# One core, a GNN and linear-attention layer with experts: V·K products and feature folds written as pairs of 64 columns or 64 rows of the TensorE array, the folds in two PSUM banks of their own

## What is computed

```python
q = split_heads(x @ Wq.T + bq)
k = split_heads(x @ Wk.T + bk)
v = split_heads(x @ Wv.T + bv)
q_prime = _feature_map(q, P)          # relu(einsum('bhsd,hmd->bhsm', t, P)) / sqrt(64)
k_prime = _feature_map(k, P)
kv = jnp.einsum('bhsm,bhsd->bhmd', k_prime, v)
attn = jnp.einsum('bhsm,bhmd->bhsd', q_prime, kv)
```

## Time and profile before

| What | us |
|---|---|
| median of 3 runs | 1213.19 (1212.43 to 1213.55) |
| the profiled execution | 1213.78 |
| its span, first to last instruction | 1211.8 |
| TensorE busy (matmuls) | 1133.4, 94% of the span |
| TensorE weight loads | 979.1, 81% |
| VectorE, ScalarE, GpSimd busy | 384.5, 250.0, 293.6 |
| folds (L1491), busy time | 34.5, 256 records |
| kv (L1574), busy time | 22.1, 160 records |

### The profile page before, as it was taken

How to read it: one execution, slowest core, us unless ns; L and a number is a source line. 1 busy time by engine, 2 the same in 40 slices (tenths; PEclk the granted TensorE clock), 3 DMA queues, 4 the chain that set the end, 5 groups by cost and what they waited for, 6 DMA issues and landing times.

```text
span 1211.8 us, 15068 instructions
## 1 busy us (share of the span) xinstructions
PE 1133.4 (94%) x5547; PEld 979.1 (81%) x5547; DVE 384.5 (32%) x1007; ACT 250.0 (21%) x388; POOL 293.6 (24%) x236
## 2 busy tenths in 40 slices
PE   3999999999999989999889986888799999999998
PEld 3886888878899988888668875667599999998887
DVE  5865255655531011322202112333532112111111
ACT  4431111112233343211101111322312211112000
POOL 5001201122132254300134423233303332216000
PEclk9999999999999999999989998999899999999999
DMA  5222001212243565512387766665103212114321
GB/s 190 96 69 96 12 18 54 68 57 70 64 129 108 196 241 197 168 41 98 89 263 221 221 178 187 196 181 165 53 2 113 70 56 64 57 56 166 121 96 70
DMA packets 143364, 139.28 MB, mean 115 GB/s; under 512 B 6507, under 2 KB 120507, under 8 KB 142012
## 3 DMA queue, kind: packets, MB, share of 16 engines
q1 hardware_dynamic: 141996, 135.51, 35.7%
q10 hardware_dynamic: 1296, 2.79, 0.6%
HBM read 102.32 MB, written 35.96 MB: 114 GB/s over the span
## 4 chain that ended last, share of the span: by engine, by line
PE 84%; DMA 6%; DVE 4%; ACT 3%; issue 2%; SPq 2%; DVEq 0%; ACTq 0%
PE ps L1481 9%; PE ps L1483 9%; PE ps L1482 9%; PE ps L1745 6%; PE ps L1747 6%; PE ps L1746 6%; DMA qs0L<-qT_d 3%; PE ps L1791 3%; PE ps L1792 3%; PE ps L1793 3%; PE ps L1661 3%; PE ps L1687 3%; PE ps L1682 3%; PE ps L1663 3%; PE ps L1662 3%; PE ps L1491 2%
## 5 line engine op out<-in xcount | busy, mean ns | idle before, releaser
L1481 PE MATMUL ps<-w_hi,xnH 128*128 128x512 f32 x480 | 192.2, 400 | 0.0
L1483 PE MATMUL ps<-w_hi,xnL 128*128 128x512 f32 x480 | 188.4, 392 | 0.0
L1482 PE MATMUL ps<-w_lo,xnH 128*128 128x512 f32 x480 | 188.2, 392 | 0.0
L1483 PEld LDWEIGHTS ps<-w_hi,xnL 128*128 128x128 f32 x480 | 90.7, 189 | 19.4
L1481 PEld LDWEIGHTS ps<-w_hi,xnH 128*128 128x128 f32 x480 | 91.2, 190 | 17.9
L1482 PEld LDWEIGHTS ps<-w_lo,xnH 128*128 128x128 f32 x480 | 91.2, 190 | 17.8
L751 POOL TENSOR_TENSOR cL<-cR,cH 128x1280 fp32r<-128x1280 f32 x20 | 58.7, 2937 | 145.5 <-ACT cH L967 132.8
L701 POOL TENSOR_TENSOR acc<-acc,cw 128x320 f32<-128x320 f32 x40 | 35.4, 884 | 172.9 <-ACT cw L873 172.1
L1604 PE MATMUL ps<-xnH,w_hi 128*128 128x416 f32 (+1 forms) x192 | 70.2, 366 | 3.4 <-DVE mL L1264 3.3
L1745 PE MATMUL ps<-x2H,guH 128*128 128x416 f32 (+1 forms) x192 | 69.4, 362 | 0.4 <-ACT wT L1046 0.4
L1747 PE MATMUL ps<-x2H,guL 128*128 128x416 f32 (+1 forms) x192 | 69.0, 359 | 0.0
(11 more groups left out here) (310 smaller groups left out, 2083.4 us busy)
## 6 DMA issues: line engine op xcount, KB each, us to landing
cR<-c_d SPq DMA_DIRECT2D x20, 640.0 KB, 4.4
foldin<-in SPq DMA_DIRECT2D x32, 256.0 KB, 2.7
guR<-in SPq DMA_DIRECT2D x16, 512.0 KB, 5.2
c_d<-cw SPq DMA_DIRECT2D x40, 160.0 KB
w_raw<-in SPq DMA_DIRECT2D x12, 512.0 KB, 6.7
xb<-in SPq DMA_DIRECT2D x10, 512.0 KB, 5.0
qs0H<-qT_d SPq DMA_DIRECT2D x10, 512.0 KB, 6.2
qs0L<-qT_d SPq DMA_DIRECT2D x10, 512.0 KB, 7.4
```

The source lines that it names most:

```text
L1481: pe.matmul(target, xnH[:, kc, cols], wH[w][:, kc, :], start=(kc == 0), stop=False)
L1482: pe.matmul(target, xnH[:, kc, cols], wL[w][:, kc, :], start=False, stop=False)
L1483: mm = pe.matmul(target, xnL[:, kc, cols], wH[w][:, kc, :], start=False, stop=(kc == KC - 1))
```

## The change

`fold` and `kv` issue eight f32 matmuls in place of four, each for one head. In `fold` a matmul has the 64 rows of its head as contraction (`tile_position` (0, 0) or (64, 0)), still 128 columns of weights, and 64 moving columns. In `kv` it has all 128 rows, but 64 columns of weights, which go to the left or the right half of the array (`tile_position` (0, 0) or (0, 64)), and 64 moving columns. The two row halves of a fold write into two different banks, which belong to the folds alone: 6 and 7 for f = 0, 0 and 1 after that. The folds leave the rotation of three banks and get semaphores of their own; a fold waits until VectorE has drained the fold before it. kv writes 64 partitions by 64 columns of bank 5 per head, and `kv_out` copies the same elements from there. The index transposes of the edge ranges move from banks 6 and 7 to 5.

```diff
@@ _job_ids
             names.append(("v", hf, t))
-            if 1 <= t <= KC:
-                names.append(("fold", hf, t - 1))
...
-        names.append(("fold", 3, j) if j < KC else ("m", (j - KC) // 2, (j - KC) % 2))
+        if j >= KC:
+            names.append(("m", (j - KC) // 2, (j - KC) % 2))
...
+        def fold_banks(f):
+
+            first = 0 if f else 6
+            return ps[:, first * BANK:(first + 2) * BANK].rearrange("q (k b) -> q k b", k=2)[:, :, 0:4 * HD]\
+                .rearrange("q k (g m) -> q k g m", g=4)
+
+        def fold_panel(w, kc):
+            return w[:, kc, :].rearrange("q (g k m) -> q k g m", g=4, k=2)
...
             def fold_high(f, kc):
-                name = ("fold", f, kc)
-                act.wait_ge(*made(name))
-                act.activation(wH[(1, 1, 0, 1)[f]][:, kc, :], job_bank(name), ACT.Copy).then_inc(fold_hi, 1)
+                act.wait_ge(fold_mm, fold_index(f, kc) + 1)
+                act.activation(fold_panel(wH[(1, 1, 0, 1)[f]], kc), fold_banks(f), ACT.Copy).then_inc(fold_hi, 1)
...
             def fold(f, kc):
-                name, n = ("fold", f, kc), fold_index(f, kc)
-                free_bank(name)
+                n, banks = fold_index(f, kc), fold_banks(f)
+                if n:
+                    pe.wait_ge(fold_lo, n)
+                else:
+                    pe.wait_ge(bias_ev, 1)
                 pe.wait_ge(in_fold[n % 2], 16 * (n // 2 + 1))
                 for g in range(4):
-                    mm = pe.matmul(job_bank(name)[:, g * P:(g + 1) * P], foldin[:, n % 2, g, :],
-                                   pbd_s[:, f % 2 * 4 + g, :], start=True, stop=True)
-                mm.then_inc(mm_done, 1)
+                    for k in range(2):
+                        own = slice(k * HD, (k + 1) * HD)
+                        mm = pe.matmul(banks[:, k, g, :], foldin[own, n % 2, g, :], pbd_s[own, f % 2 * 4 + g, own],
+                                       start=True, stop=True, tile_position=(k * HD, 0))
+                mm.then_inc(fold_mm, 1)
...
                 for g in range(4):
-                    mm = pe.matmul(bank(5)[:, g * P:(g + 1) * P], vst[:, t, g * P:(g + 1) * P],
-                                   ktmp[:, t % 2, g * P:(g + 1) * P], start=(t == 0 and g == 0),
-                                   stop=(t == NT - 1 and g == 3))
+                    for k in range(2):
+                        head = slice(g * P + k * HD, g * P + (k + 1) * HD)
+                        mm = pe.matmul(bank(5)[k * HD:(k + 1) * HD, g * HD:(g + 1) * HD], vst[:, t, head],
+                                       ktmp[:, t % 2, head], start=(t == 0 and g == 0), stop=(t == NT - 1 and g == 3),
+                                       tile_position=(0, k * HD))
                 mm.then_inc(kv_done, 1)
```

More of the change, by code:

```diff
@@ L69, in _job_ids @@
             names.append(("v", hf, t))
-            if 1 <= t <= KC:
-                names.append(("fold", hf, t - 1))
         for t in range(NT):
             names.append(("k", hf, t))
-            if hf == 1 and 1 <= t <= KC:
-                names.append(("fold", 2, t - 1))
     for j in range(24):
         names.append(("q", j))
-        names.append(("fold", 3, j) if j < KC else ("m", (j - KC) // 2, (j - KC) % 2))
+        if j >= KC:
+            names.append(("m", (j - KC) // 2, (j - KC) % 2))
     for hf in range(2):
@@ L290, in gps_layer @@
         eq = sem("eq")
+        fold_mm = sem("fold_mm")
         fold_hi = sem("fold_hi")
+        fold_lo = sem("fold_lo")
         bias_mm = sem("bias_mm")
@@ L387, in load_fold @@
                 if n >= 2:
-                    sp.wait_ge(*made(("fold", (n - 2) // KC, (n - 2) % KC)))
+                    sp.wait_ge(fold_mm, n - 1)
                 source = (wk_nat, wq_nat)[f // 2][:, f % 2 * 4:f % 2 * 4 + 4, kc * P:(kc + 1) * P]
@@ L1126, in fold_low @@
             def fold_low(f, kc):
-                name, w = ("fold", f, kc), (1, 1, 0, 1)[f]
+                w = (1, 1, 0, 1)[f]
                 dve.wait_ge(fold_hi, fold_index(f, kc) + 1)
-                dve.tensor_tensor(wL[w][:, kc, :], job_bank(name), wH[w][:, kc, :].bitcast(F32), ALU.subtract)\
-                   .then_inc(ev, 1)
+                dve.tensor_tensor(fold_panel(wL[w], kc), fold_banks(f), fold_panel(wH[w], kc).bitcast(F32), ALU.subtract)\
+                   .then_inc(fold_lo, 1)
             def edges_convert():
@@ L1159, in edges_reach @@
                 for c, col, op in ((cmax, 0, ALU.max), (cmin, 2 * P, ALU.min)):
-                    edge(dve.tensor_reduce(c[:, 0:1], bank(6)[:, col:col + P], AX_X, op))
-                    edge(dve.tensor_reduce(c[0:NCH - P, 1:2], bank(6)[0:NCH - P, col + P:col + 2 * P], AX_X, op))
+                    edge(dve.tensor_reduce(c[:, 0:1], bank(5)[:, col:col + P], AX_X, op))
+                    edge(dve.tensor_reduce(c[0:NCH - P, 1:2], bank(5)[0:NCH - P, col + P:col + 2 * P], AX_X, op))
             def edges_inside(a):
@@ L1171, in edges_ends @@
                 dve.wait_ge(range_mm, 2)
-                edge(dve.tensor_reduce(first2[:, 0:1], bank(7)[0:NWIN, 0:2 * P], AX_X, ALU.min))
-                edge(dve.tensor_reduce(first2[:, 1:2], bank(7)[0:NWIN, 2 * P:4 * P], AX_X, ALU.max))
+                edge(dve.tensor_reduce(first2[:, 0:1], bank(5)[0:NWIN, 0:2 * P], AX_X, ALU.min))
+                edge(dve.tensor_reduce(first2[:, 1:2], bank(5)[0:NWIN, 2 * P:4 * P], AX_X, ALU.max))
                 assert es[0] == EDGE_PAIR
@@ L1238, in kv_out @@
                     own = slice(k * HD, (k + 1) * HD)
-                    dve.tensor_copy(target[own, :, own], bank(5).rearrange("q (g m) -> q g m", g=4)[own, :, own])\
+                    dve.tensor_copy(target[own, :, own], bank(5, 4 * HD).rearrange("q (g m) -> q g m", g=4)[own, :, :])\
                        .then_inc(kvf, 1)
@@ L1507, in chunk_windows @@
                 for a, m in enumerate((d5F, dmin)):
-                    pe.transpose(bank(6)[:, 2 * a * P:2 * a * P + P], m[:, 0:P], ident[:])
-                    mm = pe.transpose(bank(6)[0:NCH - P, 2 * a * P + P:2 * a * P + 2 * P], m[:, P:NCH], ident[:])
+                    pe.transpose(bank(5)[:, 2 * a * P:2 * a * P + P], m[:, 0:P], ident[:])
+                    mm = pe.transpose(bank(5)[0:NCH - P, 2 * a * P + P:2 * a * P + 2 * P], m[:, P:NCH], ident[:])
                 mm.then_inc(range_mm, 1)
@@ L1516, in window_chunks @@
                         col = (2 * j + a) * P
-                        mm = pe.transpose(bank(7)[0:NWIN, col:col + P], cx[:, a, j, :], ident[:])
+                        mm = pe.transpose(bank(5)[0:NWIN, col:col + P], cx[:, a, j, :], ident[:])
                 mm.then_inc(range_mm, 1)
@@ L1582, in _ @@
                     if t == 0:
-                        pe.wait_ge(*drained(("fold", hf, KC - 1)))
+                        pe.wait_ge(fold_lo, KC * (hf + 1))
                     rows(("k", hf, t), t, 1)
@@ L1635, in _ @@
                 if j == 0:
-                    pe.wait_ge(*drained(("fold", 2, KC - 1)))
+                    pe.wait_ge(fold_lo, 3 * KC)
                 if j == 12:
-                    pe.wait_ge(*drained(("fold", 3, KC - 1)))
+                    pe.wait_ge(fold_lo, 4 * KC)
                 columns(("q", j), m, c, m // 4)
```

## The result

The changed kernel takes **1232.82 us** (median of 4 runs, 1232.04 to 1234.25); on the same chip the kernel before takes 1213.37 (1212.43 to 1214.36). The ratio is 1.0161 [1.0144, 1.0179]: slower by 19.5 us, where +8.6 was forecast, and outside the range. The profiled executions have spans of 1230.5 and 1211.8 us, +18.7; TensorE's mean granted clock is 0.976 of full speed in both.

The account below looks back on a forecast made before the run. TensorE was taken to bound the kernel. Folds at +10.4 us and kv at -1.8 gave net +8.6, which on the median of 1213.19 makes 1221.8 us; the range was 1207 to 1231, chance 0.83.

Parts of the forecast that it names:

- The direction: Whole kernel: the change makes it slower, chance 0.80.
- What bounds the kernel: From 43 to 401 us TensorE sets the time, busy 354.30 of 358.00 us, with waits of 2.5 us.
- The load sets a fold's period: In a fold, the 128-column weight load sets 0.111 us a slot; eight row pairs stay at 0.89 us.
- the rival of 1250: In folds, row halves load one after another, +0.89 us more a fold, +28.5 in all: 1250 us, chance 0.13.
- the faster ones of 1207.7, 1204 and 1190: 64-row fold loads take half: 1207.7 us, 0.10; switches free: 1204.4, or 1190 if folds halve too, 0.04.
- The switch: Going in and out of part-array form, tail included, costs 0.35 us before f32 work, 0.30 before edge matmuls.
- Kv: Each kv in column pairs takes 0.45 + 0.35 us in place of 0.89: -0.09, twenty times -1.8 us.
- the rivals of 1231 and 1213: Kv's column halves don't overlap over eight pairs: 1231 us, 0.04; the switch costs half: 1213 us, 0.06.
- "Banks and semaphores ... All zero": Fold banks, semaphore waits, ScalarE and VectorE copies and edge transposes together change the time by zero.
- The sum: Prices added per operation: folds +10.4 us, kv -1.8 us, net +8.6 us.
- No later stage gives the shift back: Behind 401 us TensorE waits only for its own results, so no later stage returns any of the shift.
- The rival of more half-clock stretches: Emptier array in folds and kv lowers the clock more often; five more stretches give +8.5 us: 1230, chance 0.05.

Follow-up runs that it names:

- split_full: Changed kernel with each fold matmul over all 128 rows, sixteen records of 64 moving columns and no part-array form; 1245.88 us.
- kv_only: Kernel before with only kv written as column pairs, folds as before; 1209.69 us, ratio 0.9983 to the kernel before.
- Loads_in_rows: Changed kernel with the edge windows' register loads issued ahead of the seventh of eight chunks of the step's row matmuls; 1214.83 us, ratio 1.0015.
- mixed: Changed kernel with half of each fold over all 128 rows and the other half as row pairs behind it; 1242.23 us.
- quarters: Loads_in_rows with each fold in 64 x 64 tiles, four side by side, 32 records; 1203.25 us, ratio 0.9927 to the kernel before.
- behind_late: Changed kernel with the fold behind its step's edge windows and VectorE's low copy of a fold behind the next step's one-hots; 1217.42 us.

## Why the prediction was wrong

- **The direction** (slower, 0.80): right, and for a part of the reason; the array's part of +8.6 is in the result.
- **What bounds the kernel**: right. TensorE sets the time from 43 us on. But the 2.5 us of waits were read as room to spare, when 2.3 of them were this very wait, L1562 for issue, the kernel already at the edge.
- **The load sets a fold's period**: right. 0.112 us a slot, with row pairs (shown) and over full height (split_full, 0.11). Row halves run together, so the rival of 1250 falls, and the faster ones of 1207.7, 1204 and 1190 with it.
- **The switch**: right in the main. A fold costs +0.30 to +0.35 beside f32 matmuls, forecast 0.35, and +0.25 ahead of edge windows, forecast 0.30; that is some 1 us less in all. **Kv**: right, -0.08 each, forecast -0.09, and kv_only's ratio agrees. So the rivals of 1231 and 1213 fall too.
- **"Banks and semaphores ... All zero"**: the step that failed. It weighed the waits of TensorE for other engines and the copies, and these are indeed nothing. Left out was TensorE's own sequencer: 16 short records in place of 8 take the same array time but twice the places of its lead, so the lead ahead of the windows fell from 3.1 to 1.0 us, against 1.9 us that each window needs. The count alone makes that 1.6; the last 0.6 stays open. The sum priced a fold from the last matmul ahead of it to the first behind it; this cost came later, inside the windows. Cost: +11.0 us in the second K pass (12.7 less 1.7) and +5.6 in the second V pass (8.0 less 2.4), 16.6 together. Loads_in_rows takes 17.7 us away with no change of the array's work, and split_full and mixed show that the lead goes by the count of records.
- **No later stage gives the shift back**: wrong by some 6 us, 1.3 at the step of 256 us, 3.4 of half clock before 500 us and 1.1 of waits for qF. The rival of more half-clock stretches doesn't hold: two fewer up to 500 us, others behind it, and 58.0 us at half clock in the whole of both executions. Why the clock no longer falls at those two places was not tested.
- **The rivals**: none held. All were about the array (halves, switch, clock), none about the engine's front end, though the row named "issue". The sum of the profile is 8.6 + 16.6 - 4.7 in what was given back (1.3 and 3.4) = 20.5. Against it stand the 0.8 us ahead at the first fold and the 1.1 of waits for qF, which makes 18.6 of +18.7; that it comes out so closely is luck, since the 8.6 are a forecast and were some 1 us less.

The Trainium skill ("TensorEngine Tiling (Array Packing)", Theoretical Speedup) promises up to twofold for a dimension of 64. The runs show that row halves bring no gain (0.88 us for a fold became 1.04) and quarters less than twofold (0.63). Its rule (Key Properties) that tiles load and multiply in parallel holds: eight pairs take 0.97 us where eight single loads take as much.

## What to carry to other kernels

Before an operation is split into more and shorter instructions, look at what TensorE's sequencer must do behind it. Its lead was a number of records here, so register loads, branches and asserts behind some 17 short records can stall an array that has work enough. A wait for "issue" on the bounding engine, 2.3 us of 358 here, was the sign that the lead was used up; put register loads where long instructions stand ahead. Compare the sequencer's own times with a run in which it isn't late before you read a delay from them. For small f32 tiles split the weight's columns, not only its rows.

## What was not expected of the hardware

- The sequencer's lead was 17 records ahead of the array in four mixes: 3.1 us with eight full fold records in it, 2.2 with sixteen of 64 moving columns, 2.0 across a change of form, and 4.07 us (at 252.5 us of the kernel before) with row matmuls alone. It was not 17 everywhere: in a fold of row pairs 14 and in one of quarters 20 had not started. Pairs and fours start together, which moves the count by one to three; the rest of the difference is open.
- A register load from memory takes the sequencer 0.30 us in the median, but single ones took up to 0.8 us in the changed kernel and 1.5 in behind_late. A window takes it 1.9 us with its register work and loop.
- Four 64 x 64 tiles load side by side: 0.69 us for 32 records.
